# Cross attention of a decoder kernel: scores on 32-row tiles, probabilities turned two slots later, values summed by four heads

## What is computed

```python
q = x @ Wq.T + bq                  # (100, 256), 16 heads of 16
k = ctx @ Wk.T + bk                # (361, 256)
v = ctx @ Wv.T + bv                # (361, 256)
p = softmax(q_h @ k_h.T * 16**-0.5)        # for each head h: (100, 361)
o = concat_h(p @ v_h)
x = layernorm(x + o @ Wo.T + bo)   # without gain and bias
```

## Time and profile before

| | us |
|---|---|
| median of 3 runs | 3083.74 (3075.91 to 3084.32) |
| the profiled execution: its own time | 3084.47 |
| its span (first to last instruction) | 3082.7 |
| PE busy | 2467.7 (80%) |
| DVE busy | 1723.8 (56%) |
| ACT busy | 1187.7 (39%) |
| POOL busy | 433.1 (14%) |
| mean granted TensorE clock | 0.894 of full |

### The profile page before, as it was taken

The page is one execution under the profiler, slowest core; times in us unless marked ns, Lnnn a source line. Parts: engine busy times, 40 slices in busy tenths (PEclk is TensorE's granted clock), DMA queues, the critical chain, the costliest instruction groups (busy, mean ns, idle before and its releaser), DMA issues. The chain is left out here.

```text
span 3082.7 us, 44584 instructions
## 1 busy us (share of the span) xinstructions
PE 2467.7 (80%) x15278; PEld 1459.9 (47%) x15279; DVE 1723.8 (56%) x3404; ACT 1187.7 (39%) x2418; POOL 433.1 (14%) x360
## 2 busy tenths in 40 slices
PE   3777777774999999876777489999999999994793
PEld 1333333332666666553444145554455544553572
DVE  3899999993555555534777234444544454453123
ACT  1666666663333333222444124343343433440110
POOL 1333333220111111002343000000000000001102
PEclk9888888885999999977787699999999999995897
DMA  3000000000000000200000200000000000006111
GB/s 110 1 1 0 0 0 0 0 0 27 13 13 10 14 10 10 68 4 9 0 0 0 72 5 11 5 5 5 5 10 5 5 5 5 5 1 229 40 32 51
DMA packets 50289, 60.41 MB, mean 20 GB/s; under 512 B 9764, under 2 KB 44889, under 8 KB 49770
## 3 DMA queue, kind: packets, MB, share of 16 engines
q1 hardware_dynamic: 47218, 53.69, 5.5%
q0 software_dynamic: 3008, 5.91, 0.7%
HBM read 51.06 MB, written 8.52 MB: 19 GB/s over the span
## 5 line engine op out<-in xcount | busy, mean ns | idle before, releaser
L1880 PE MATMUL la_side<-la_wkv,la_inT 128*128 128x512 f32 (+1 forms) x512 | 258.0, 627 | 49.2 <-DVE la_v L2004 48.3
L2138 ACT ACTIVATE la_pr<-la_pS,la_nm 100x461 f32<-100x461 f32 x256 | 163.1, 644 | 267.9 <-DVE la_nm L2041 267.9
L1868 PE MATMUL la_side<-la_inT,la_wkv 128*128 128x461 f32 x512 | 240.1, 592 | 7.6 <-ACT la_kT L2125 6.9
L2038 DVE TENSOR_REDUCE la_nm<-la_pS 100x2 f32<-100x922 f32 x128 | 142.7, 1115 | 182.9 <-PE la_pS L1899 182.9
L300 PE MATMUL sa_pS<-sa_qT,sa_kTm 128*100 128x400 f32 x512 | 195.1, 504 | 7.3 <-DVE sa_L L471 7.3
L2004 DVE COPY la_v<-la_side 128x512 f32<-128x512 f32 (+1 forms) x128 | 87.7, 685 | 180.1 <-PE la_side L1880 180.0
L895 PE MATMUL ca_pS<-ca_kT,ca_qTm 128*100 128x361 f32 x512 | 187.0, 488 | 0.5 <-DVE ca_va L974 0.5
L1075 ACT ACTIVATE ca_pr<-ca_pS,ca_nm 100x361 f32<-100x361 f32 x256 | 129.7, 559 | 125.2 <-DVE ca_nm L1009 125.1
L1006 DVE TENSOR_REDUCE ca_nm<-ca_pS 100x2 f32<-100x722 f32 x128 | 116.3, 908 | 96.6 <-PE ca_pS L895 96.5
L604 ACT ACTIVATE sa_L<-sa_L 100x800 f32<-100x800 f32 x128 | 111.3, 870 | 146.8 <-DVE sa_L L471 146.8
L1880 PEld LDWEIGHTS la_side<-la_wkv,la_inT 128*128 128x128 f32 (+1 forms) x512 | 82.3, 180 | 163.6 <-DVE la_v L2004 91.5
(11 more groups left out here) (385 smaller groups left out, 4924.1 us busy)
## 6 DMA issues: line engine op xcount, KB each, us to landing
rf_w<-in_L_ffn_W SPq DMA_DIRECT2D x16, 1024.0 KB, 13.3
ca_cn<-in_ctx SPq DMA_DIRECT2D x16, 256.0 KB, 2.7
la_cn<-in_ctx SPq DMA_DIRECT2D x16, 256.0 KB, 2.7
rows_in<-io_zero SPq DMA_DIRECT2D x20, 128.0 KB, 4.6
rb_xr<-rows_in POOLq DMA_DIRECT2D x20, 128.0 KB, 2.2
rows_out<-rb_yr SPq DMA_DIRECT2D x20, 128.0 KB, 1.7
ea_wc<-in_L_ffn_conv_W SPq DMA_DIRECT2D x1, 2048.0 KB
la_wkv<-in_L_xattn_Wkv SPq DMA_DIRECT2D x1, 2048.0 KB
```

Of the source, the lines that this page charges most:

```text
L1868: last = nc.tensor.matmul(pf[:, 0:SK], wkv[:, k, e * P:(e + 1) * P], inT[:, k, :], start=k == 0, stop=k == KD - 1)
L1880: last = nc.tensor.matmul(pf[0:keys[c], :], inT[:, k, c * P:c * P + keys[c]], wkv[:, k, o:o + 512], start=k == 0, stop=k == KD - 1)
L2038: nc.vector.reduce_max(nm[m % 2][:], pS[0:T, 2 * (m % 2):2 * (m % 2) + 2, 0:SK], AX)\
L2138: ins = nc.scalar.activation(pr[m % 2][:, e, 0:SK], pS[0:T, 2 * (m % 2) + e, 0:SK], ACT.Exp, bias=nm[m % 2][:, e:e + 1], scale=SCALE, accu ...
```

## The change

Six parts, all in `cross_attention`:

1. **Scores on row tiles of 32.** A pair's two heads are taken so that they lie in different strips of 32 rows (`pair`), and the matmul contracts over 32 rows only: `rows_` of `qTm` and `kT`. A strip holds two heads (16 rows each), so `qTm` holds q twice instead of eight times, with a mask of two columns, `odd` instead of `hmask`. The scale 1/4 is multiplied into the mask once, so DVE's maxima are negated as they are taken and the second DVE instruction of each pair goes away.
2. **Turning two slots behind.** In slot m PE now issues the scores of pair n and the turning of pair n-2 (it was n-1). `pr` has NP = 4 buffers for two.
3. **Values by four heads.** In every odd slot PE sums pairs n-5 and n-4 together: 12 matmuls, ordered so that four in a row write four different strips of PSUM rows. `pT` has four buffers for two.
4. **Evacuation shared.** DVE copies `pPT` in even slots, ACT in odd slots, behind the exponentials of the pair of that slot.
5. **Side steps placed anew** (`SLOTS`). The scores of a batch wait for fk0 and later fk1 by themselves, and the values for all fronts; bo's division is written as two products, since the heads now lie in another order.
6. **Start.** DVE waits for the small loads first, scales the mask and zeroes four `pr` buffers; POOL waits for DVE.

```diff
     MP = NH // 2
+    MQ = MP // 2
+    QR = 32
+    NT = P // QR
+    pair = lambda m: [HG * (m // 4) + 4 * (m % 2) + 2 * e + m % 4 // 2 for e in range(2)]
-    SLOTS = [["fx"], ["fc0", "fq"], ["fc1", "bo"], ["bp", "fv0"], ["fk0", "by"], ["fk1", "fv1"], [], []]
-    NORM = 6
+    SLOTS = [["fx", "fc0"], ["fc1", "fq"], ["fk0"], ["fk1"], ["fv1", "bo"], ["bp"], ["by"], ["fv0"]]
+    NP = 4
...
                 def scores(i, b, m):
                     n = i * MP + m
+                    if m % 4 == 0:
+                        pe.wait_ge(s_R, side.read_of(i, f"fk{m // 4}"))
                     if m == 0:
-                        pe.wait_ge(s_R, side.front_done(i))
                         pe.wait_ge(s_qm, i + 1)
                     above(pe, s_P, n - 1)
-                    for e in range(2):
-                        h = 2 * m + e
-                        last = nc.tensor.matmul(pS[0:T, 2 * (m % 2) + e, 0:SC], qTm[b][:, h // HG, h % HG, :],
-                                                kT[b][:, h // HG, :], start=True, stop=True)
+                    for e, h in enumerate(pair(m)):
+                        t = h % HG // 2
+                        rows_ = slice(QR * t, QR * (t + 1))
+                        last = nc.tensor.matmul(pS[0:T, 2 * (m % 2) + e, 0:SC], qTm[b][rows_, h // HG, h % 2, :],
+                                                kT[b][rows_, h // HG, :], start=True, stop=True)
...
                 def values(n, i, b, m):
+
                     pe.wait_ge(s_PT, n + 1)
-                    if m == 0:
+                    if m == 1:
+                        pe.wait_ge(s_R, side.front_done(i))
                         above(pe, s_av, i)
-                    for e in range(2):
-                        h = 2 * m + e
-                        j = h % 4
-                        for c in range(NC):
-                            last = nc.tensor.matmul(pav[32 * j:32 * j + 32, (h // 4) * T:(h // 4 + 1) * T],
-                                                    va[b][:, c, h, :], pT[m % 2][:, e, c * T:(c + 1) * T],
+                    four = [(k, e, h) for k in (m - 1, m) for e, h in enumerate(pair(k))]
+                    for c in range(NC):
+                        for k, e, h in four:
+                            j = h // 2 % 4
+                            last = nc.tensor.matmul(pav[32 * j:32 * j + 32, (m // 2) * T:(m // 2 + 1) * T],
+                                                    va[b][:, c, h, :], pT[k % 4][:, e, c * T:(c + 1) * T],
                                                     start=c == 0, stop=c == NC - 1)
...
                         scores(i, b, m)
-                        for part in (turned_pair, summed_pair, None):
-                            if small:
-                                name, n = small.pop(0)
-                                step(name, n, i + 1 if name[0] == "f" else i - 1, 1 - b)
-                            if part:
-                                part(i, b, m)
+                        between()
+                        if m >= 2 or not first:
+                            turn(n - 2, (m - 2) % MP)
+                        between()
+                        if m >= 5 and m % 2:
+                            values(n - 4, i, b, m - 4)
+                        elif m % 2 and not first:
+                            values(n - 4, i - 1, 1 - b, MP - 4 + m)
...
-                    nc.vector.reduce_max(nm[m % 2][:], pS[0:T, 2 * (m % 2):2 * (m % 2) + 2, 0:SC], AX)\
+                    nc.vector.reduce_max(nm[m % 2][:], pS[0:T, 2 * (m % 2):2 * (m % 2) + 2, 0:SC], AX, negate=True)\
                         .then_inc(s_mx, 1)
-                    dv.wait_ge(s_mx, 2 * n + 1)
-                    nc.vector.tensor_scalar(nm[m % 2][:], nm[m % 2][:], -SCALE, None, ALU.mult).then_inc(s_mx, 1)
...
                 ch.base, ch.n = 0, 0
+                dv.wait_ge(s_w, 16 * NW)
+                ch.after(nc.vector.tensor_scalar(odd[:], odd[:], SCALE, None, ALU.mult))
                 for b in range(2):
                     ch.after(nc.vector.memset(va[b][:], 0.0))
...
+                for b in range(NP):
                     ch.after(nc.vector.memset(pr[b][:], 0.0))
...
                         exps(i, m)
-                        if m == NORM and behind:
+                        if m % 2 and (m >= 3 or not first):
+                            evac(n - 2, i * MQ + (m - 1) // 2 - 1, (m - 2) % MP)
+                        if m == MP - 1 and not first:
                             rstd(i - 1)
...
-                            qTm[b][:, e, :, :], qb[:, e, :].unsqueeze(1).broadcast_to([P, HG, T]),
-                            hmask[:, :].unsqueeze(2).broadcast_to([P, HG, T]), ALU.mult)
+                            qTm[b][:, e, :, :], qb[:, e, :].unsqueeze(1).broadcast_to([P, 2, T]),
+                            odd[:, :].unsqueeze(2).broadcast_to([P, 2, T]), ALU.mult)
```

More of the change, by code:

```diff
@@ L1083, in body @@
                 def body(i, b):
+                    first = isinstance(i, int) and i == 0
                     for m in range(MP):
-                        behind = not (isinstance(i, int) and i == 0)
+                        n = i * MP + m
                         small = side.steps(i, m)
-                        for name, n in small[:1]:
-                            step(name, n, i + 1 if name[0] == "f" else i - 1, 1 - b)
-                        if m == 2 and behind:
+                        for name, k in small[:1]:
+                            step(name, k, i + 1 if name[0] == "f" else i - 1, 1 - b)
+                        if m == 4 and not first:
@@ L1090, in body @@
                             sums(i - 1)
                         exps(i, m)
[L1092 removed]
+                        if m % 2 and (m >= 3 or not first):
+                            evac(n - 2, i * MQ + (m - 1) // 2 - 1, (m - 2) % MP)
+                        if m == MP - 1 and not first:
                             rstd(i - 1)
[L1094 to L1095 removed]
+                        for name, k in small[1:]:
+                            step(name, k, i + 1 if name[0] == "f" else i - 1, 1 - b)
```

88 lines of the change are left out of this document (47 added, 41 removed).

## The result

| | before | after |
|---|---|---|
| median of the runs, us | 3080.8 (3075.9 to 3084.3, 4 runs) | 2974.4 (2968.1 to 2982.8, 4 runs) |
| ratio, 95% interval | | 0.967 (0.964 to 0.970) |
| span of the profiled execution, us | 3082.7 | 2981.1 |
| cross attention: first to last instruction, us | 543.1 | 436.5 |
| a batch at full clock, fx to fx, us | 32.0 | 24.2 |

The change is 3.3% faster, 106 us; the forecast was 2986. The table of windows, the kernel after: one batch, then the stages of the cross attention, the expert adapter and the bucket attention.

A forecast was written before the change was run, and what follows sets the result against it. TensorE's instructions one after the other were taken to bound a 32.0 us batch; 23.2 of work plus 2.3 of waits gives 25.5, so 3084.5 - 104 + 6 = 2986.5 us, forecast 2986, range 2952 to 3032.

The forecast's parts named there:

- Scores: Score matmuls on 32-row tiles: 0.78 us a slot for 1.29, next group 0.105 dearer; 3.2 us a batch won.
- The rival of the strict order: Score records start only in program order: three periods for two, 0.30 a slot, 3006 to 3025; 5 in 100.
- Values: Value matmuls by four heads: 0.63 us every second slot for 0.83 every slot; 4.1 us a batch won.
- PE's work: TensorE's work in a batch without waits: 30.5 - 3.2 - 4.1 = 23.2 us.
- Waits: PE standing for other engines: 2.3 us a batch for 1.5, bounds 0 and 4; the least sure term.
- the two smaller ones: Waits of fc0 behind fx's copy and of bo behind fv1's read: 0.6 us a batch together.
- the base of 0.65: Wait before fc1: ACT's context copy is done at 3.5 us, PE wants fc1 at 2.85.
- up to 0.65 more where DVE still normalises: Extra wait before fc1 while DVE normalises the batch before; wait there put at 1.1 us in all.
- 6.5 x 16: Whole stage: 6.5 us saved a batch (25.5 for 32.0) in all 16 batches, 104 us less.
- Prologue: Stage start: DVE waits for loads before zeroing four buffers; 6.4 us later, 0.5 back, 6 us of loss.
- The other stages: 0: Stages outside the cross attention aren't touched, so they change by 0.
- The clock: Rival: PE, less dense at 91%, loses full clock; slower 3 in 100, faster but over 3010 7 in 100.

The follow-up runs named there:

- the run with 128 rows: The changed kernel, but each score matmul contracts over all 128 rows again under a mask of eight columns; 3007.1 us, 0.979.
- the run in head order: The changed kernel, but the 12 value matmuls of four heads stand head by head instead of block by block; 3001.2 us, 0.979.
- the fastest version: The changed kernel with ScalarE's context copy ahead of slot 0's exponentials and the zeroing before the wait for the loads; 2954.3 us, 0.962.
- two neighbours: The changed kernel with two probability buffers for four (3009.0 us, 0.978), and the changed kernel turning one slot behind instead of two (3023.6 us, 0.983).
- the tiles alone: The kernel before with only the 32-row score tiles and two-column mask; old order, values pair by pair, two buffers; 3033.7 us, 0.988.
- the zeros first: The changed kernel, but DVE zeroes its buffers before waiting for the small loads and scaling the mask; 2974.7 us, 0.966.

## Why the prediction was right, point by point

**Scores.** The forecast's price was 0.78 for 1.29, from two tiles of 64 rows; measured 0.783. The four records start at 904.079, 904.086, 904.463 and 904.470: two and two, across the heads. The trace doesn't say which head a record is of, but with both heads on one tile they start 0.30 apart, so the two that start together are of different heads. The rival of the strict order, priced with a head's two records side by side, falls: its three periods would be 0.91 us, and the whole slot takes 0.78. The Trainium skill (TensorE: Matmul & The Clock Gate, "The mechanism") has matmuls start and end in strict order. If an fp32 matmul's two records count as two matmuls there, this trace disagrees; if they count as one, it agrees (the heads' first records start 0.007 us apart, the second ones too). No run here decides which. The group behind was to pay 0.105 more; the rows give 0.10 for groups of 128 columns (1.32 at L864 for the 1.22 of the run with 128 rows) but 0.05 for fx and bp, 0.08 on the mean. So 8 x (1.29 - 0.78 - 0.08) = 3.4, for 3.2.

**Values.** 0.63 was forecast, 0.67 measured, so 4.0 for 4.1. But the reason was half the story: by the run in head order, the grouping of two pairs alone gave 1.7 of it.

**PE's work.** 24.23 less the waits is 22.8, for 23.2; 0.2 of that is the smaller loss behind the scores, the rest is not assigned.

**Waits.** The ones named were there, in the order named, and all too large: fc1 0.78 on the mean for 1.1, fq 0.19 for 0.2, bp 0.21 for 0.4, the two smaller ones together (0.16 and 0.06) 0.2 for 0.6. 1.4 for 2.3. At fc1 the base of 0.65 was right (0.59 where the normalising is out of the way, in the run with all evacuations on VectorE), and the step that failed is "up to 0.65 more where DVE still normalises": the normalising delays the maximum by 0.27 at most (903.29, where 0.21 behind the scores' end would be 903.02).

**A batch** is 24.2 for 25.5, a gain of 7.8 for 6.5. That would be 124 us for 16, and it was 114.5 from the first fx to the stage's end (the 106.6 of the stage and the 7.9 of the prologue, below), for the forecast's 104. The step "6.5 x 16" hid a second error of the other sign: the period holds from the third fx to the last, 13 times (415.9 to 314.7: 101 us). The first two intervals went from 50.3 to 44.8, partly at the lower clock, and the stretch from the last fx to the end from 64.2 to 56.3: 13 us for three batches, where 23 would be the full gain. Part of the rest is the clock. The second batch and the stretch behind the last fx, after, and the same stretch before:

```profile
782.10:806.19 24.09, 22.25 (x153) 13.27 (x153) 11.14 (x15) 11.81 (x24) 2.02 (x4) 0.86 0.06 17
1120.90:1175.50 54.60, 46.95 (x476) 30.25 (x474) 27.50 (x49) 26.37 (x56) 2.40 (x4) 0.89 0.00 1
1221.60:1284.10 62.50, 58.62 (x445) 40.35 (x443) 35.49 (x69) 21.40 (x47) 4.41 (x4) 0.99 0.00 0
```

A mean of 0.86 over 24.1 us and of 0.89 over 54.6 cost 3.4 and at most 6 us (estimates, by the half of PE's speed that is missing). The forecast came so near by sizes that were off and in part cancelled: that is luck, where the list of terms was right.

**Prologue.** 6 us later was forecast, and the first fx is 5.9 later, but this too is luck: the whole stage began 1.9 us earlier in this execution. The first copy of turned weights and what follows, after:

```profile
740.72 0.58 ACT L763 COPY ca_L_xattn_Wq_T<-cat_turn 128x512 f32<-128x512 f32 x1 [7.86 <-PE cat_turn L755]
...
752.48 0.17 DVE L1041 TENSOR_SCALAR ca_odd<-ca_odd 128x2 f32<-128x2 f32 x1 [19.18 <-DMA ca_odd<-in_c_odd]
...
760.65 0.07 DVE L1050 MEMSET ca_rc<- 100x16 f32 x1
...
761.33 0.57 PE L853 MATMUL ca_side<-io_ident,ca_xs 100*128 100x100 f32 x2 [15.28 <-POOL ca_xs L1135]
```

The same copy stood at 742.66 before. From it to the first fx are 20.6 us for 12.7: 7.9 lost, where the forecast's sum has 6.4. The loads came as long behind it as before (11.8 for 11.6); the scaling and the zeroings with the gaps between them took 8.2 us for the forecast's 7.5 (a zeroing costs 0.92 from start to start, not 0.75); and GpSimd's staging of x, which now waits for them too, stands behind them with 0.54 that the sum left out.

**The other stages: 0.** They gave back 7 us behind the stage in this execution (132.0 for 130.1, 284.2 for 280.4 and 1 us in the gaps and stages after), at a lower mean clock in these two. In the fastest version they are 120.0 and 279.9, with the same instructions and a mean clock of 0.90 and 0.76 for 0.80 and 0.73: the adapter alone moves by 12 us with the granted clock. What sets it there is open. So the profiled execution gained 101.6 us where 98 were forecast: 8.6 more in the stage, 2 more ahead of it, 7 less behind it.

**The clock.** It did not fall in the steady batches: PEclk is 1.00 from the third fx to the last. At both ends of the stage it did, as shown above, and the stage's mean is 0.93 for 0.97; "PEclk still at full in the stage" holds for the loop only. The rival got 10 in 100 for both its sides, and for this kernel that was fair; but two neighbours lost some 20 and 30 us of their loops by it (the sum of what their batches took over 25.1 and, an estimate, 24.8 us). The rival's measure, work over period, was 91% in the forecast; in the runs it orders them, but closely (94% in the change and 93% with the tiles alone; 92% with two buffers and 91% turning one slot behind). The length of the longest wait tells them apart more clearly: 0.9 and 0.7 us against 1.4 and 1.3.

## What to carry to other kernels

Two heads on different row tiles of 32 cost little more than one: 0.78 for 1.29 us, and the whole of it is overlap, since on one tile they take 1.38. But count what both neighbours pay for the change of shape, and look at the order first: here order, delay and two pairs in one go were worth 3.3 us a batch, each kind of tile 2.2 to 2.3.

When PE is the bound and almost never idle, read the longest single wait of a batch, not the sum: ask who holds it and whether that engine could do the one short copy first. That edit was four lines, took away 0.8 us a batch, and 41 us of the kernel with two buffers.

Multiply a period by the number of times the timeline shows it, and treat the first and the last batch apart. Compare starts by a fixed instruction of the stage, not by the clock of the whole execution.

## What was not expected of the hardware

A single idle stretch of PE of 1.1 to 1.4 us, in the steady batches of a stage otherwise dense, was followed within 2 us by the lower clock in 20 of 27 cases (seven of 14 and 13 of 13), for some 3 to 14 us; stretches of 0.6 to 0.9 in one of 56 (14 each of the change, the evacuations on VectorE, the zeros first and the values head after head). It is no rule for the ends of the stage: in the second batch of the change the clock fell at 784.8 without such a stretch, and with the tiles alone it stood through one of 1.4 in the last batch (to 1230.0, the clock at full to 1237.6). With both heads on one tile the clock fell for some 45 us with no idle stretch before it, once in the loop; nothing here explains that.

Behind a turning, scores of the same shape cost 1.21 us for 1.29 behind values: the change of shape is paid only where the shape does change.

24 value records head after head took 1.24 us, less than two groups of twelve (1.66), though they are the same instructions.
